# A token tower of 32 pairs: the looped programs of four engines written out pair by pair

## The reference, cut to what matters

```python
h = tok(x)            # layernorm, conv2d + relu, three times; layernorm; res @ out_w + out_b
h = h + attn(_layernorm(h))
h = h + ffn(_layernorm(h))

def attn(x):          # 64 images, 128 tokens, 8 heads of width 64
    q, vf, vb = split(x @ wqv_w.T + wqv_b)
    k = x[:, :, None, :] * wk[None, None]
    a = -sum_w |q[b,s,h,:] - k[b,t,h,:]| / sqrt(w)      # L1 scores, all s x t
    a = softmax(concat([a, 0], axis=1), axis=1)[:, :t]
    o = sum over heads of (a applied to vf, and transposed a applied to vb)
    return x + (o * sigmoid(1.702 * o)) @ fanin_w.T + fanin_b

def ffn(x):           # each token goes to the one of 32 experts with the largest logit
    idx = argmax(x @ router_w.T + router_b)
    return relu(relu(x @ W1[idx] + b1[idx]) @ W2[idx] + b2[idx])
```

## Time and profile before

| | |
|---|---|
| median of 3 runs | 3506.68 us (3501.89 to 3508.08) |
| the profiled execution | 3508.91 us, span 3507.0 us |
| TensorE busy | 92% of the span |
| VectorE | 88% |
| GpSimd | 81% |
| ScalarE | 78% |
| DMA queue of GpSimd (the halves of absd) | 501.51 MB, 72.0% of 16 engines' span |
| mean granted clock of TensorE | 0.986 |

### The profile page before, as it was taken

How to read it: one execution, slowest core, us unless ns; L and a number is a source line. 1 busy time by engine, 2 the same in 40 slices (tenths; PEclk the granted TensorE clock), 3 DMA queues, 4 the chain that set the end, 5 groups by cost and what they waited for, 6 DMA issues and landing times. The chain is left out here.

```text
span 3507.0 us, 78749 instructions
## 1 busy us (share of the span) xinstructions
PE 3243.3 (92%) x23140; PEld 2458.9 (70%) x23140; DVE 3086.9 (88%) x4389; ACT 2723.1 (78%) x4859; POOL 2856.5 (81%) x2792
## 2 busy tenths in 40 slices
PE   8899999999999999999999999999999999999888
PEld 6676777776777777677767777766777777777555
DVE  5888889998898989988999889989989999989886
ACT  3777787887787877877788878778778788777875
POOL 2888888888888888888888888878888888888885
PEclk8999999999999999999999999999999999999999
DMA  6778777787787787777888877877777887778884
GB/s 135 154 153 164 155 155 153 157 162 156 151 163 154 157 161 158 158 150 153 161 160 159 160 153 156 164 149 157 157 155 157 166 159 157 154 158 160 163 159 86
DMA packets 199653, 543.63 MB, mean 155 GB/s; under 512 B 69142, under 2 KB 133398, under 8 KB 146744
## 3 DMA queue, kind: packets, MB, share of 16 engines
q0 software_dynamic: 73728, 501.51, 72.0%
q1 hardware_dynamic: 125880, 41.54, 5.9%
HBM read 10.93 MB, written 2.10 MB: 4 GB/s over the span
## 5 line engine op out<-in xcount | busy, mean ns | idle before, releaser
L925 DVE TENSOR_REDUCE S<-psU 128x16 f32<-128x1024 f32 x2183 | 2604.4, 1217 | 297.8 <-PE psU L486 281.3
L486 PE MATMUL psU<-flat,kT 99*128 99x256 bf16 x16384 | 2304.1, 275 | 212.5 <-ACT absd L711 102.9
L711 ACT ACTIVATE absd<-psU 128x1024 f32<-128x1024 f32 x1913 | 1936.7, 1023 | 554.3 <-PE psU L486 541.0
L486 PEld LDWEIGHTS psU<-flat,kT 99*128 99x128 bf16 x16384 | 1495.6, 98 | 855.2 <-DVE S L925 219.3
L1194 POOL TENSOR_TENSOR absd<-absd 128x1024 f32<-128x1024 f32 (+2 forms) x512 | 1179.8, 2304 | 248.9 <-DMA absd<-absd 245.0
L1198 POOL TENSOR_TENSOR absd<-absd 128x512 f32<-128x512 f32 (+2 forms) x512 | 610.3, 1192 | 40.2
L1183 POOL DMA_DIRECT2D absd<-absd x512 | 454.2, 887 | 200.4 <-ACT absd L711 145.2
L1201 POOL TENSOR_TENSOR absd<-absd 128x256 f32<-128x256 f32 (+2 forms) x512 | 351.7, 687 | 40.1
L498 PE MATMUL psC<-c1in,w 128*128 128x384 f32 (+1 forms) x930 | 309.4, 415 | 0.8 <-DVE c1in L969 0.8
L590 PE MATMUL psZ<-P,v 128*128 128x256 f32 x1024 | 288.6, 384 | 0.0
L517 PE MATMUL psC<-c3in,w 128*128 128x128 f32 x1240 | 251.8, 287 | 1.7 <-DVE c3in L969 1.7
(11 more groups left out here) (180 smaller groups left out, 2231.3 us busy)
## 6 DMA issues: line engine op xcount, KB each, us to landing
absd<-absd POOLq DMA_DIRECT2D x412, 1024.0 KB, 7.9
absd<-absd POOLq DMA_DIRECT2D x65, 768.0 KB, 6.5
flat<-qparts SPq DMA_DIRECT2D x3072, 8.0 KB, 4.1
absd<-absd POOLq DMA_DIRECT2D x35, 512.0 KB, 4.9
xin<-in_x SPq DMA_DIRECT2D x32, 192.0 KB, 8.0
flat<-pattern SPq DMA_DIRECT2D x4, 768.0 KB, 10.9
out_h<-result SPq DMA_DIRECT2D x32, 64.0 KB, 6.0
w<-in_w SPq DMA_DIRECT2D x1, 1280.0 KB
```

What stands on the lines that cost most here:

```text
L486: mm = nc.tensor.matmul(psU[:, slot % PLACES, m], kT[0:ROWS + 3, b, m, :], flat[0:ROWS + 3, half % HALVES, :, lo:lo + BLOCK], start=True, ...
L711: nc.scalar.activation(absd[:, c % GROUPS, :, u], psU[:, slot % PLACES].rearrange("p (n a) s w -> p n (a s w)", n=2), ACT.Abs).then_inc(a_ ...
L925: nc.vector.tensor_reduce(S[:, b, hd, SB * c:SB * c + SB], psU[:, slot % PLACES].rearrange("p a s w -> p s a w"), AX.XY, ALU.add, apply_ab ...
```

## The change

program() gets a switch, and the four engines throw it: pairs 1 to 29 are then made by a Python loop that emits each pair's instructions, with the pair's number as a constant. The order of work on each engine stays. SyncE's program, which doesn't go by program(), keeps its loop.

```diff
-        def program(eng, prologue, iteration, epilogue):
+        def program(eng, prologue, iteration, epilogue, looped=True):
 
             prologue()
             iteration(0, late=False)
-            with eng.Fori(1, PAIRS - 2) as i:
-                iteration(i)
+            if looped:
+                with eng.Fori(1, PAIRS - 2) as i:
+                    iteration(i)
+            else:
+                for i in range(1, PAIRS - 2):
+                    iteration(i)
             iteration(PAIRS - 2, tokens=False)
             iteration(PAIRS - 1, tokens=False, ahead=False)
             epilogue()
...
-            program(pe, prologue, iteration, epilogue)
+            program(pe, prologue, iteration, epilogue, looped=False)
...
-            program(act, prologue, iteration, epilogue)
+            program(act, prologue, iteration, epilogue, looped=False)
...
-            program(dve, prologue, iteration, epilogue)
+            program(dve, prologue, iteration, epilogue, looped=False)
...
-            program(pool, prologue, iteration, epilogue)
+            program(pool, prologue, iteration, epilogue, looped=False)
```

## The result

The changed kernel takes 3567.68 us (median of 4 runs, 3556.34 to 3576.14) against 3507.38 us (4 runs, 3501.89 to 3514.65) for the kernel before, measured beside it: a ratio of 1.0177, 95% interval 1.0158 to 1.0195. It is slower by some 60 us; the forecast was 3540 us in a range of 3499 to 3600.

The account below looks back on a forecast made before the run. A ring of engines with little slack, no one bound engine. Register work and waits -6, packet hits on group 13 +28, other flights +11: +33 us on 3508.91, forecast 3540 us by the median, range 3499 to 3600.

Parts of the forecast that it names:

- (a): TensorE's loop branch, 208 ns at each pair's start, is covered by the wait for psU: gain 0.
- Rival 3: Back edges did cost an instruction fetch, so writing out saves 24 us: 3483 us; chance 0.03.
- (b): ScalarE's register work between two waits goes: 0.08 us sooner each, 0.8 us a pair if half waited on the path.
- (c): TensorE's fourth slots: late wait becomes its own instruction, load 0.07 us later, 0.7 us a pair if all on path.
- (d): TensorE's 16 KB instruction packets delay group 13's DMA on GpSimd: 12 of 28 pairs, 2.33 us each, +28 us.
- rival 4: Every pair hit, or each hit brings the low clock: +116 us, 3623; half is 3565; chance 0.15 for 3580 to 3630.
- (e): GpSimd waits longer for its other DMAs: 0.4 us a pair, +11 us; bounds 0 and 2.2 a pair.
- Rival 2: Packets absorbed in GpSimd's wait at group 13's tree: 3498 to 3513 us, likeliest 3501; chance 0.22.
- Rival 5: An engine runs out of instructions, its packet late in full queues; TensorE idles: 3550 to 3600 us; chance 0.05.

Follow-up runs that it names:

- e3: Kernel before with TensorE's loop body holding two pairs instead of one, register waits kept: 3674.15 us, ratio 1.0491.
- e10: Kernel before with ScalarE's two waits in a group's first unit swapped, buffer first and matmuls last: 3506.44 us, ratio 0.9994.
- e4: Changed kernel with TensorE's two waits in fourth slots swapped, place of psU first and queries' load second: 3553.50 us, ratio 1.0143.
- e1: Kernel before with TensorE's program alone written out, the other three engines keeping their loop: 3561.75 us, ratio 1.0167.
- e7: Changed kernel with layernorm statistics in slot 1, shift in slot 2, and trees 13 slots after their group instead of 11: 3552.41 us, ratio 1.0148.
- e12: Changed kernel with layernorm statistics and shift in slot 1 and trees 12 slots after their group instead of 11: 3526.18 us, ratio 1.0060.
- e5: Kernel before plus six 16 KB DRAM copies a pair from SyncE, which were cut into 1 KB packets: 3536.59 us, ratio 1.0090.
- e11: Kernel before with layernorm statistics and shift in slot 1 and trees 12 slots after their group instead of 11: 3497.48 us, ratio 0.9972.

## Why the prediction was right

Sign, mechanism and order of size were right, the count of late additions in part by luck; the size was 28 us short by the medians (3567.68 against 3540) and 14 us short by the profiled execution (3556.34 against 3541.9).

(a) The branch for nothing: held. Pair 2's first load of the changed kernel comes 1.00 us after the one before it ended, against 0.96 and 1.02 in the earlier trace rows. Rival 3, the back edges costing 24 us, is out, and e3 shows what it would have looked like. The Trainium skill (Runtime: NRT & Kernel Launch, Instruction fetch mechanics) says that a taken branch to a target outside the window waits for a fetch. e3 agrees, with 5.7 us for each; the earlier trace rows show that the kernel before was not such a case. The section also says that crossing into the next block is mostly hidden and that kernels prefer to be unrolled. For TensorE's own stream no row of the changed kernel speaks against the first; the second was wrong here by 60 us, since the packets fell on others' transfers.

(b) and (c): the delays are as read, 0.08 us less for ScalarE (0.116 to 0.037 behind TensorE at the queries' part) and 0.06 more for TensorE. Neither shows in the time of e10 or surely in that of e4. A fourth slot of the changed kernel, TensorE's load 0.12 us behind VectorE's end (1183.15 + 1.22 = 1184.37), as in pair 30 of the earlier trace rows:

```profile
1183.15 1.22 DVE L929 TENSOR_REDUCE S<-psU 128x16 f32<-128x1024 f32 x1
...
1184.49 0.35 PEld L490 LDWEIGHTS psU<-flat,kT 99*128 99x128 bf16 x4 [0.44 <-issue]
```

A net of -6 us was within the bounds, and 0 is as good.

(d) The hits. Six packets of 16 KB in nearly every pair, (187 - 25) / 28 = 5.8. Group 13 landed in 8.0 us or more with such a packet in flight in 11 of 28 pairs; 12 were forecast from 8 / 18. That the two agree is luck, for two errors cancel. A packet was in flight in 19 pairs and not 12, and eight of the 19 landed in 7.2 to 7.9 us, while the forecast counted every packet in flight as a hit. Nor did the packets drift through the pairs, as was assumed: seven pairs (5, 10, 11, 15, 16, 21, 27) had a late group 13 in all five kernels whose TensorE is written out (changed, e1, e4, e7, e12). All eleven passes behind the late ones show ScalarE idle over 1 us at line 764, and so do three others (pairs 4, 14 and 15), two of them (4 and 15) behind a group 12 that took 8.8 and 8.7 us. Not all fourteen are new: pairs 4, 14 and 21 had such a wait in the kernel before too, of 1.03, 1.37 and 1.87 us, with the clock at 0.50 behind it and no packet. The eleven passes average 109.99 us against 106.71 for a pass of the kernel before: 3.28 us for a hit instead of 2.33, so 36 us instead of 28. The step that was mis-sized is the price, taken from pairs 1 and 2 of which only one had the slow clock; it fell in 10 of the 11. (The eleventh took 108.72 us. Against the same eleven passes before, 106.35 us on average, it is 3.64 us each, 40 in all.) This is a part of rival 4, which was weighed as if all or none fell: the clock fell in 12 of the 28 passes, before in 4. Its sum, 3580 or more, was not reached.

(e) The rest. The other 17 passes average 107.53 us, 0.82 more than 106.71, in all 14 us; forecast were 0.4 a pair for (e), 11 us, less 6 for (b) and (c). So the sum by the forecast's terms is 36 + 14 = 50 us where 33 stood. What was missing in (e) is its second route. Its 0.4 us had been put near the lower bound because the busy times of pair 1 hardly show more, but a wait is idle time, which a busy time can't show. I had priced it only from GpSimd's waits, which rose from 203.8 to 250.8 us in 28 passes, 9.0 a pair, at the low end of the forecast (9 to 11). The flat loads, which TensorE waits for in person, were not looked at: 4.4 us of that wait before and 18.0 after on the matmuls. That they are the larger part of the 14 us is an argument from e5 and e12, not shown by itself.

Rival 2, the packets absorbed, was to be decided by group 13 at 7.2 to 7.5 us with a packet in flight. It went up to 9.6, but six of the 19 flights did land in 7.2 to 7.5 us. As a forecast of the time rival 2 is out; of a packet in flight it holds in six cases of 19. Rival 5, TensorE out of instructions: its loads do wait longer for nothing that the profile shows, 49.6 before and

```profile
PEld psU L490 <- issue: 176.1, 411, 1.5
```

after. This is a change of label rather than of time. In fourth slots the late wait is now an instruction of its own, so the load behind it has no releaser in the profile (as at 3288.42 in the earlier trace rows). The waits of that line for VectorE and ScalarE fell from 219.3 + 214.6 to 123.5 + 169.1 us at the same time.

Not explained: why the profiled execution of the changed kernel lies 11 us under its median, so that 60 us by the medians are 47 in rows. The passes with the low clock are a likely place, and the profile shows one execution only; the mean granted clocks of the four executions, 0.976, 0.972, 0.975 and 0.969 for 3556, 3566, 3569 and 3576 us, bear it out in part. Nor is it known what decides whether a packet in flight makes an addition late.

## What to carry to other kernels

Where the pace hangs on large DMA transfers that land just in time, a loop whose body needs no instruction packets can be worth more than what its branch and register work cost, as it was here. Look at the instruction queues of the profile first, by stretch: a body without packets is a reason to be wary of writing it out or making it longer. A hole of up to 2.2 us cost 3.3 us a pass here, and TensorE's clock fell behind it in ten passes of eleven; so find the one wait by which the delay reaches TensorE, and move what it waits for earlier, as e11 does.

## What the runs showed of the hardware that was not expected

A packet of 16 KB took 0.9 to 1.7 us (median 1.05), and with one in flight a 1 MB addition that otherwise lands in 7.2 us landed in anything from 7.2 to 9.6 us. In the late ones of pairs 4 and 5 fifteen of the sixteen updates were on time and one was late, by up to 2.3 us. That is more than the packet's own time; why is open. In the five latest flights (9.3 to 9.6 us) the packet began 7.3 to 7.4 us after the issue, when the other updates had nearly all come, while three that began at 6.9 to 7.1 us changed nothing. A contiguous copy of 4096 fp32 numbers was cut into 16 packets of 1 KB, while one of 4093 numbers went as a single packet, and the two cost 0.37 and 0.78% at the same place. A loop of one pair on TensorE ran 28 passes without a fetch, and one of two pairs, some 3200 instructions, fetched anew in every pass and stood 4.3 to 7.3 us at the back edge (5.7 on average).
